# Routers' logits in column groups, and one block for the LoRA experts' norm, router and spreading

## What is computed

```python
probs = jax.nn.softmax(x @ W_r.T + b_r, axis=-1)        # 8 experts
w_topk, idx_topk = jax.lax.top_k(probs, 2)
base1 = x @ W1.T + b1                                   # 256 -> 1024
u1 = jnp.einsum('nd,erd->ner', x, A1)                   # rank 8 for each of 8 experts
for k in range(2):
    oh = jax.nn.one_hot(idx_topk[:, k], E)
    z1 = (u1 * oh[:, :, None]).reshape(N, E * R)
    h = act(base1 + z1 @ B1_rf * SCALING)
    z2 = (einsum('nf,erf->ner', h, A2) * oh[:, :, None]).reshape(N, E * R)
    res = res + w_topk[:, k:k + 1] * (h @ W2.T + b2 + z2 @ B2_rf * SCALING)
```

## Time and profile before

| | us |
|---|---|
| median of 3 runs | 3330.79 (3326.05 to 3331.14) |
| the profiled execution | 3341.11 |
| its span in the profile | 3339.2 |
| TensorE matmuls busy | 2849.8 |
| VectorE busy | 1869.3 |
| ScalarE busy | 1424.1 |
| LoRA stage, first instruction to first matmul of its main loop | 1421.0 to 1494.2 |
| sparse stage L0, first mean to first logits instruction on VectorE | 559.5 to 587.9 |
| sparse stage L3, the same | 3009.7 to 3036.3 |

### The profile page before, as it was taken

The page is one execution under the profiler, slowest core; times in us unless marked ns, Lnnn a source line. Parts: engine busy times, 40 slices in busy tenths (PEclk is TensorE's granted clock), DMA queues, the critical chain, the costliest instruction groups (busy, mean ns, idle before and its releaser), DMA issues. The chain is left out here.

```text
span 3339.2 us, 47277 instructions
## 1 busy us (share of the span) xinstructions
PE 2849.8 (85%) x17584; PEld 1764.4 (53%) x17588; DVE 1869.3 (56%) x2411; ACT 1424.1 (43%) x2534; POOL 915.0 (27%) x742
## 2 busy tenths in 40 slices
PE   7999987989977987779997976557989798898897
PEld 5788863456654655543344632223654455554786
DVE  2333325412228945624458959667965799995332
ACT  3333325112236635432155645346557666652122
POOL 0111110013302522100003500000540799980462
PEclk9999998989989988979998988779999899998998
DMA  4000000501120000020000000000000111103124
GB/s 142 0 0 0 0 7 21 176 26 46 45 77 1 2 21 2 2 81 0 0 19 1 2 13 0 0 20 1 2 28 14 75 74 75 76 32 103 54 81 139
DMA packets 72275, 121.74 MB, mean 36 GB/s; under 512 B 10721, under 2 KB 53217, under 8 KB 71586
## 3 DMA queue, kind: packets, MB, share of 16 engines
q1 hardware_dynamic: 63170, 94.86, 8.5%
q0 software_dynamic: 8928, 24.39, 2.3%
HBM read 100.48 MB, written 18.74 MB: 36 GB/s over the span
## 5 line engine op out<-in xcount | busy, mean ns | idle before, releaser
L2933 POOL TENSOR_TENSOR h<-ssm_u,ss_bc 128x1024 f32<-128x1024 f32 x88 | 205.7, 2359 | 0.0
L2896 ACT ACTIVATE ssm_p_h<-ss_delta,ss_decay 128x256 f32<-128x256 f32 x352 | 146.5, 463 | 123.7 <-DVE ctxT L2970 83.8
L2845 PE MATMUL ssm_p_y<-ctxT,ident 128*128 128x512 f32 x412 | 187.8, 596 | 0.0
L573 POOL TENSOR_TENSOR xw_prob<-xw_prob,xw_rsum 128x1024 f32<-128x1024 f32 x32 | 60.7, 1897 | 418.6 <-DVE xw_rsum L560 418.6
L553 DVE TENSOR_REDUCE xw_nmax<-xw_p_s 128x8 f32<-128x1024 f32 x32 | 39.2, 1225 | 237.1 <-PE xw_p_s L484 237.1
L1379 POOL MEMSET ctxT<- 128x512 f32 x3 | 1.6, 527 | 588.1 <-POOLq L60 588.1
L2965 DVE TENSOR_TENSOR_SCAN ssm_p_h<-ssm_p_h,h 128x1024 f32<-128x1024 f32 x64 | 145.8, 2279 | 8.5 <-ACT ssm_p_h L2896 6.8
L2923 POOL TENSOR_TENSOR ctxT<-ctxT,ss_bc 128x1024 f32<-128x1024 f32 x50 | 117.5, 2357 | 15.4 <-DVE ctxT L2963 15.4
L2829 PE MATMUL ssm_p_h<-ssm_b_diagonal,ssm_uT 128*128 128x128 f32 x640 | 85.0, 289 | 40.6 <-DVE ctxT L2970 19.5
L2845 PEld LDWEIGHTS ssm_p_y<-ctxT,ident 128*128 128x128 f32 x412 | 76.5, 192 | 79.5 <-issue 78.3
L461 PE MATMUL xw_p_q<-h,xw_m_h 128*128 (+1 forms) x1024 | 117.0, 275 | 1.3 <-PEq L60 1.3
(11 more groups left out here) (716 smaller groups left out, 7209.5 us busy)
## 6 DMA issues: line engine op xcount, KB each, us to landing
ss_bc<-ss_bc_rows SPq DMA_DIRECT2D x24, 896.0 KB, 4.3
ss_bc<-ss_bc_rows SPq DMA_DIRECT2D x8, 768.0 KB, 3.9
L3f_rows<-L3f_rows_out SPq DMA_DIRECT2D x16, 384.0 KB, 3.9
L0f_wg<-in_L_ffn_gate SPq DMA_DIRECT2D x9, 512.0 KB, 9.7
L0f_wu<-in_L_ffn_up SPq DMA_DIRECT2D x9, 512.0 KB, 9.4
L0f_wd<-in_L_ffn_down SPq DMA_DIRECT2D x9, 512.0 KB, 10.4
L0f_rows<-L0f_rows_out SPq DMA_DIRECT2D x16, 256.0 KB, 4.1
x<-in_xT SPq DMA_DIRECT2D x1, 2048.0 KB, 7.3
```

Of the source, the lines that this page charges most:

```text
L573: g.tensor_tensor(prob[:, :, :], prob[:, :, :], bcast(rsum[:, 1, :], 2, S2), ALU.mult).then_inc(sem["normed"], 1)
L2845: mm = pe.matmul(p_y[:, 2 * half:2 * half + 2, :].rearrange("p e t -> p (e t)"), k.ident[:, :], weighed[n % RING_W][:, ts(half, CH)], star ...
L2896: i = act.activation(out[:, ts(e, CT)], delta[:, e, ts(c, CT)], ACT.Exp, scale=decay[:, E4 * s + e:E4 * s + e + 1])
L2933: g.tensor_tensor(tiles(drive[n % RING]), u[:, c % 2, :, :], bcast(bcs[:, row_b(s), :], 1, E4), ALU.mult).then_inc(sem["driven_g"], 1)
```

## The change

A class `Logits` takes the place of the logits matmuls in all three routers. `products(c)` makes the logits of a quarter as four products of 128 tokens in four column groups of TensorE's array: `w_r`, now padded to 32 columns, is the stationary operand, the tokens the moving one, and each group writes 32 partitions. `copied(c)` moves the 128x128 result to SBUF on ScalarE, `turned(c)` transposes it back, so that VectorE finds tokens on the partitions with a stride of 32.

In the LoRA stage the blocks of `layer_norm`, `router` and `lmp_` become one block `lmf_`. The norm is `Norm` with one bank; logits and the products with `a1` stand between its steps; the low-rank products are copied to `z` by ScalarE. After the picks the routes (32 columns for each token, cleared by GpSimd) are turned by plain matmuls with the identity, in four column groups, into four copies of 32 rows; `select` (the four old selectors, 32 rows each) then spreads them with four matmuls on four row groups. ScalarE copies the two weights out of PSUM, VectorE multiplies the change mask into `z` and copies the mask. The main loop's wait for the wide weights moves to its own start. The diff, cut:

```diff
+class Logits:
...
+    def __init__(self, k, ctx, sem, ln, w_r, slots, p_l):
+        self.k, self.sem, self.ln, self.w_r, self.slots, self.p_l = k, sem, ln, w_r, slots, p_l
+        self.flat = sb(k, ctx, "raw_logits", [P, 2, P])
+    def products(self, pe, c):
+        pe.wait_ge(self.ln.sem["ln_normed"], c + 1)
+        n = len(self.slots)
+        if c >= n:
+            pe.wait_ge(self.sem["raw_copied"], c - n + 1)
+        for a in range(H2):
+            for q in range(4):
+                mm = pe.matmul(self.slots[c % n][32 * q:32 * q + 32, :], self.w_r[:, a, :], self.k.h[:, a, c * CH + q * P:c * CH + q * P + P],
+                               start=a == 0, stop=a == H2 - 1, skip_group_check=True)
+        mm.then_inc(self.sem["raw"], 1)
+    def copied(self, act, c):
+        act.wait_ge(self.sem["raw"], c + 1)
+        if c >= 2:
+            act.wait_ge(self.sem["logits"], c - 1)
+        act.copy(self.flat[:, c % 2, :], self.slots[c % len(self.slots)]).then_inc(self.sem["raw_copied"], 1)
+    def turned(self, pe, c):
+        pe.wait_ge(self.sem["raw_copied"], c + 1)
+        pe.transpose(self.p_l[:, ts(c, P)], self.flat[:, c % 2, :], self.k.ident[:, :]).then_inc(self.sem["logits"], 1)
...
-def router(k, wT, rows, w_r, s_w, n_w, E, top, add_bias=None, rank_bias=None, separate=False):
...
-                def logits(c):
-                    pe.wait_ge(sem["ln_normed"], c + 1)
-                    for t in range(4 * c, 4 * c + 4):
-                        for a in range(H2):
-                            mm = pe.matmul(p_l[:, t, :], k.h[:, a, ts(t, P)], w_r[:, a, :], start=a == 0, stop=a == H2 - 1, skip_group_check=True)
-                    mm.then_inc(sem["logits"], 1)
...
                 pe.wait_ge(s_r, n_r)
-                logits(0)
+                lo.products(pe, 0)
                 ln.var(pe, 2)
-                logits(1)
+                lo.products(pe, 1)
+                lo.turned(pe, 0)
                 ln.var(pe, 3)
-                logits(2)
-                logits(3)
+                lo.products(pe, 2)
+                lo.turned(pe, 1)
+                lo.products(pe, 3)
+                lo.turned(pe, 2)
+                lo.turned(pe, 3)
...
-            sp.dma_start(a1[:, :, :], k.dram[L + "A1T"].rearrange("(a p) e -> p a e", p=P)).then_inc(s_w, 16)
-            sp.dma_start(pick[:, :, :], k.dram[L + "pick"]).then_inc(s_w, 16)
-            sp.dma_start(pick_w[:, :, :], k.dram[L + "pick_w"]).then_inc(s_w, 16)
+            sp.dma_start(a1[:, :, :], k.dram[L + "A1T"].rearrange("(a p) e -> p a e", p=P)).then_inc(s_a, 16)
+            sp.dma_start(select[:, :], k.dram[L + "select"]).then_inc(s_a, 16)
...
-        layer_norm(k, k.x, k.h, prefetch)
-        k.prefix = "lm_"
-        router(k, rT, ROWS, w_r, s_r, 32, E, 2, add_bias=br[:, :], separate=True)
...
+            res = sb(k, pre, "routes", [P, NT, 32])
+            p_n = ps(k, pre, "p_n", [P, 2, CH])
+            p_lt = ps(k, pre, "p_l", [P, CH])
+            p_l = p_lt[:, :].rearrange("p (t e) -> p t e", e=32)[:, :, 0:E]
+            p_raw = ps(k, pre, "p_raw", [P, CH])
+            ln = Norm(k, pre, sem, k.x, k.h, own=(sb(k, pre, "square", [P, 2, H2, CH]), sb(k, pre, "rstd", [P, 2, CH]), p_n[:, 0:1, :], p_n[:, 1:2, :]))
+            lo = Logits(k, pre, sem, ln, w_r, (p_raw[:, 0:P],), p_lt)
...
+                def low(c):
+                    for a in range(H2):
+                        mm = pe.matmul(p_k[:, c, :], a1[:, a, :], k.h[:, a, ts(c, CH)], start=a == 0, stop=a == H2 - 1)
+                    mm.then_inc(sem["low"], 1)
+                def turn(c):
                     if c >= 2:
-                        pe.wait_ge(sem["done"], c - 1)
-                    for a in range(H2):
-                        mm = pe.matmul(p_a[:, c % 2, :], a1[:, a, :], k.h[:, a, ts(c, CH)], start=a == 0, stop=a == H2 - 1)
-                    mm.then_inc(sem["low"], 1)
+                        pe.wait_ge(sem["routed"], c - 1)
+                    for t in range(4):
+                        for r in range(4):
+                            mm = pe.matmul(p_n[32 * r:32 * r + 32, c % 2, ts(t, P)], res[:, 4 * c + t, :], k.ident[:, :], start=True, stop=True, skip_group_check=True)
+                    mm.then_inc(sem["turned"], 1)
+                def spread(c):
+                    pe.wait_ge(sem["routed"], c + 1)
+                    if c >= 1:
+                        pe.wait_ge(sem["weights_read"], c)
+                        pe.wait_ge(sem["rest_read"], c)
+                    else:
+                        pe.wait_ge(sem["low_copied"], NCH)
+                    for r in range(4):
+                        mm = pe.matmul(p_k[:, r, :], select[32 * r:32 * r + 32, :], rT[32 * r:32 * r + 32, ts(c, CH)], start=True, stop=True)
+                    mm.then_inc(sem["selected"], 1)
+                ln.mean(pe, 0)
+                ln.mean(pe, 1)
+                ln.var(pe, 0)
+                ln.mean(pe, 2)
+                ln.var(pe, 1)
+                ln.mean(pe, 3)
+                pe.wait_ge(s_r, 32)
+                lo.products(pe, 0)
+                ln.var(pe, 2)
+                pe.wait_ge(s_a, 32)
+                low(0)
+                lo.turned(pe, 0)
+                lo.products(pe, 1)
+                ln.var(pe, 3)
+                low(1)
+                lo.turned(pe, 1)
+                lo.products(pe, 2)
+                low(2)
+                lo.turned(pe, 2)
+                lo.products(pe, 3)
+                low(3)
+                lo.turned(pe, 3)
+                pe.wait_ge(sem["picked"], 1)
+                turn(0)
+                turn(1)
+                spread(0)
+                turn(2)
+                spread(1)
+                turn(3)
+                spread(2)
+                spread(3)
...
+                def low_copied(c):
+                    act.wait_ge(sem["low"], c + 1)
+                    act.copy(z[:, ts(c, CH)], p_k[:, c, :]).then_inc(sem["low_copied"], 1)
+                def routed(c):
+                    act.wait_ge(sem["turned"], c + 1)
+                    act.copy(rT[:, ts(c, CH)], p_n[:, c % 2, :]).then_inc(sem["routed"], 1)
+                def weights(c):
+                    act.wait_ge(sem["selected"], c + 1)
+                    act.copy(wb[:, 0, ts(c, CH)], p_k[:, 2, :])
+                    act.copy(wb[:, 1, ts(c, CH)], p_k[:, 3, :]).then_inc(sem["weights_read"], 1)
...
+                lo.copied(act, 0)
+                ln.inverse(act, 2)
+                low_copied(0)
+                lo.copied(act, 1)
+                ln.inverse(act, 3)
+                low_copied(1)
+                lo.copied(act, 2)
+                low_copied(2)
+                lo.copied(act, 3)
+                low_copied(3)
+                act.wait_ge(sem["shifted"], 1)
+                act.activation(pr[:, :, :], lg[:, :, :], ACT.Exp).then_inc(sem["exped"], 1)
+                routed(0)
+                routed(1)
+                weights(0)
+                routed(2)
+                weights(1)
+                routed(3)
+                weights(2)
+                weights(3)
...
+                v.wait_ge(sem["logits"], NCH)
+                chain(v.tensor_tensor(vals[:, :, :], p_l, bcast(br[:, :], 1, NT), ALU.add))
...
-                    v.wait_ge(sem["copied"], 4 * c + 1)
-                    v.wait_ge(sem["low"], c + 1)
-                    v.scalar_tensor_tensor(out=z[:, ts(c, CH)], in0=p_a[:, c % 2, :], scalar=2.0, in1=change[:, c % 2, :], op0=ALU.mult, op1=ALU.mult).then_inc(sem["done"], 1)
+                    v.wait_ge(sem["selected"], c + 1)
+                    v.wait_ge(sem["low_copied"], c + 1)
+                    v.scalar_tensor_tensor(out=z[:, ts(c, CH)], in0=z[:, ts(c, CH)], scalar=2.0, in1=p_k[:, 0, :], op0=ALU.mult, op1=ALU.mult)
+                    v.tensor_copy(mk[:, ts(c, CH)], p_k[:, 1, :]).then_inc(sem["rest_read"], 1)
...
+            pe.wait_ge(s_w, 96)
...
-    d[L + "pick"], d[L + "pick_w"], d[L + "bias2"] = pick.reshape(P, 2, P), pick_w, bias2
+    pick = pick.reshape(P, 2, P)
+    d[L + "select"] = c(np.concatenate([pick[0:32, 0], pick[0:32, 1], pick_w[0:32, 0], pick_w[0:32, 1]], axis=0))
+    d[L + "bias2"] = bias2
```

177 lines of the change are left out of this document (71 added, 106 removed).

## The result

The changed kernel takes 3306.97 us (median of 6 runs, 3300.57 to 3307.98) against 3330.97 for the kernel before, run beside it: a ratio of 0.9929, 95% interval 0.9916 to 0.9942. The forecast was 3309.5 in a range of 3301 to 3320, with 0.96 for faster by over 0.2%. On another chip the same two kernels gave 0.9932 (0.9921 to 0.9944).

A forecast was written before the change was run, and what follows sets the result against it. TensorE, busy 85% of 3339.2 us, was taken as the bound, so changes pay where it waits, works on little or runs at half clock. 18.4 - 1.0 + 1.3 + 2.6 = 21.3 off 3330.8 gave 3309.5, range 3301 to 3320.

The forecast's parts named there:

- Logits, +1.3 and +2.6: Sparse-expert stages: column-group logits let VectorE start earlier, gaining 1.3 us in L0 and 2.6 in L3.
- The norm, a loss of 5.9 (24.7 to 26.3): LoRA stage: the one-bank norm takes 25.5 us, within 24.7 to 26.3, and ends 5.9 later than before.
- Behind the norm, VectorE 4.2 late: LoRA block: VectorE starts routing 4.2 us behind the norm's end, with two low-rank products, 3.4 us, on the path.
- Turning and spreading, 14.5 (12 to 19): LoRA block behind the picks: turning and spreading routes in groups ends 14.5 us after them, bounds 12 to 19.
- Clock back after 5 us: Turning and spreading: TensorE starts at half clock after VectorE's chain and returns to full clock after 5 us.
- The loop's start, 1.0 lost (0 or 2): Main loop behind the LoRA block: a half-clock start loses 2 us, otherwise none; 1.0 was taken.
- The sum, 21.3: Whole kernel: LoRA gain 18.4, less 1.0 at the loop, plus 1.3 and 2.6 in sparse stages, gives 21.3 us.
- 10.3 above the median: Profiled execution of before: 10.3 us over the runs' median, none tied to these stages, so 21.3 is taken from 3330.8.
- (a): Rival: clock stays low through spreading, partly behind the norm and at the loop's start; gain 13.8, 3317 us; chance 0.17.
- (b): Rival: gains more, with clock back early, one slow mean, no loop loss; gain 26.3, 3304.5 us; chance 0.11.
- (c): Rival: groups do not run together in turning and spreading; gain about 8, 3323 us; chance 0.04.
- (d): Rival: slower, main loop stays at half clock; 43 us of that cancels the gain, 60 gives 3339; chance 0.02.

The follow-up runs named there:

- low products late: Changed kernel with the third and fourth low-rank products moved behind the last turned logits, their copies behind ScalarE's exp; ratio 0.9930 to the kernel before.
- Filled: Changed kernel plus dummy matmuls that nothing reads, nine while VectorE routes and one on either side of the last spread; ratio 0.9929 to the kernel before.
- Held: Changed kernel with late low-rank products, four mean banks and dummy matmuls, including extra ones at the block's end and ahead of the main loop; ratio 0.9911, median 3297.77 us.
- second profile: The changed kernel itself, unaltered, run again on a third chip beside the kernel before; ratio 0.9932, median 3302.92 us.
- whole-array kernel: Changed kernel with routes turned by transposes and four 32-row selectors applied one after the other, without row or column groups; ratio 0.9998 to the kernel before.

## Why the prediction was right, point by point

- **Logits, +1.3 and +2.6**: up to VectorE's start, where they were summed, 1.0 and 2.6; up to the first expert product 1.8 and 3.1. The products cost 0.64, as costed; VectorE starts 1.45 behind the last scaling, where 1.3 and 1.7 were costed. In L3 the clock did not fall, which the 1.7 allowed for. That both gains "pass on whole" was too little: the row transposes behind them left half clock as well, which the sum does not have, and gave 0.8 and 0.5 more.
- **The norm, a loss of 5.9 (24.7 to 26.3)**: 26.3, the range's very end, in the first profile, with two means at half clock; 24.4 in most others of the one-bank norm, with one, just under the range. Against 19.6 that is a loss of 6.7 or 4.8. The mechanism held; the two outcomes were seen, and the forecast took their middle.
- **Behind the norm, VectorE 4.2 late**: 4.5. The estimate that two low-rank products stand on the path was right (without them VectorE starts 1.9 behind the norm), and low products late shows that they need not.
- **VectorE's chain, 8.3**: 8.3.
- **Turning and spreading, 14.5 (12 to 19)**: 14.2, by the mechanism foreseen, but two terms were off and cancel in part. The first spread starts 0.7 sooner than costed (3.6 against 4.3). Each spread takes 1.14 where 0.86 was costed: the attention output had 2.9 of its 18.73 us at half clock, for 16 records, so the other 112 took 0.14 each, not 0.11, and at 0.14 eight of them are 1.13. So the spreads stand 2.64 apart, not 2.4 to 2.5. That the end came within 0.3 is partly luck. VectorE's two reads took 0.69 and 0.69 where 0.69 and 0.69 were taken, and the mask copy, in no row of before, lay between its bounds of 0.425 and 0.85. The Trainium skill's warning in "TensorEngine Tiling (Array Packing)", PSUM Bottleneck, holds here with a period of 2.64 against 1.2 of TensorE's work. It doesn't follow that the groups give nothing: 14.2 stands against 23.3 for the same block on the whole array with 128 rows, a comparison that the prediction did not make.
- **Clock back after 5 us**: 4.1 in the first profile (the turns from 1455.12 are slow, the second spread is not). Filled puts the price of that half clock at 1.9.
- **The loop's start, 1.0 lost (0 or 2)**: 2.2. Here the size was off: two outcomes were named, the worse one came, and the sum had their mean, which neither gives. TensorE's hole of 3.6 ahead of the loop, against 2.83 before, did bring half clock, and for 5 us. Held shows the cause, a hole ahead of the loop, and the remedy.
- **The sum, 21.3**: by the traces 17.4 in front of the loop, less 2.2 in it, plus 1.8 and 3.1, is 20.1, where the medians differ by 24.0; the interval of the ratio reaches from 19.3 to 28.0. The changed kernel's second profile, with one slow mean, gives 17.2 for LoRA, 2.6 and 3.1 for the sparse stages: 22.9, where the medians on its chip differ by 23.1. So of the 4 us that lack, about 2 are the second slow mean of the first profile, and nearly 1 lies in L0. The rest is not settled; both sums stand on the one profile of before, and stages that no kernel changed scatter by as much: between the kernels that have the new logits in L0 the first mean of LoRA stands anywhere from 1412.0 to 1416.8.
- **That the profiled execution of before was 10.3 above the median for reasons outside these stages**: its loop over L3's experts took 10.3 longer than the changed kernel's (the first of its products stands 23.9 later, the last 34.2), and nothing in it was changed. From that loop's first product to its last it took 179.6 there, 174.7 to 178.5 in the four profiles of the chip on which the kernel before has a median of 3337.11, and 169.0 to 169.8 in the nine others: its length goes with the chip and not with the change. To go by the median was right.
- **Rivals**: (a) clock low throughout, did not come for this kernel; the whole-array kernel, with other products, shows what it can cost, 22 us more up to the last copy. (b), 3304.5, is as near to the median as the forecast, but its reasons did not come together: the clock returned 0.9 us sooner than forecast, one slow mean came in the second profile and not in the first, and the loop's start lost more, not less. That the median, 3306.97, lies midway between the forecast and (b) tells nothing for either. (c) the groups do run together (64 records in 3.64 at mostly half clock, 8 in 1.14). (d) the loop lost 2.2 and came back.
